# VectorE makes the inverse roots of the second layer's norms for the first four turns, in place of GpSimd

## The reference

```python
x = x + _L1_ffn_ref(_layernorm(x), ...)            # gates by attention over 524288 edges, 4 experts, 2 chosen
x = x + _L2_gnn_ref(_layernorm(x), adj, ...)       # inside: x + relu((adj @ h) @ W_rel + b + h @ W_root), h = layer_norm(x, gamma, beta)
x = x + _L2_ffn_ref(_layernorm(x), ...)            # a shared expert and 2 of 8 experts for each row
x = x + _L3_gnn_ref(_layernorm(x), mask, adj, W)
x = x + _L3_ffn_ref(_layernorm(x), ...)            # 2 of 8 experts for each row
def _layernorm(x): return (x - mean(x)) / sqrt(var(x) + 1e-5)
```

## Time and profile before

| | |
|---|---|
| time, median of 3 runs | 2797.84 us (2797.29 to 2801.29) |
| the profiled execution | 2798.21 us, span 2796.4 us |
| mean granted TensorE clock | 0.897 of full speed |
| busy in the span: PE, DVE, ACT, POOL | 2234.9, 1778.3, 1368.1, 1307.3 us |

### The profile page before, as it was taken

The page is one execution under the profiler, slowest core; times in us unless marked ns, Lnnn a source line. Parts: engine busy times, 40 slices in busy tenths (PEclk is TensorE's granted clock), DMA queues, the critical chain, the costliest instruction groups (busy, mean ns, idle before and its releaser), DMA issues. The chain is left out here.

```text
span 2796.4 us, 40730 instructions
## 1 busy us (share of the span) xinstructions
PE 2234.9 (80%) x12080; PEld 1656.4 (59%) x12080; DVE 1778.3 (64%) x4734; ACT 1368.1 (49%) x3026; POOL 1307.3 (47%) x1219
## 2 busy tenths in 40 slices
PE   4989898999999897888605156588999989999990
PEld 2544545464555554655405155588988979889880
DVE  5999989777788575333476852766465585744512
ACT  3554647474756553555404053465546545444440
POOL 1011100100010575567755777416737767667776
PEclk9999999998999998999857577799999999999995
DMA  4010104000010214222231212345536554566662
GB/s 154 1 40 1 32 12 96 16 17 20 13 32 1 54 29 124 79 76 77 60 122 50 76 39 72 84 124 146 136 92 161 157 153 129 145 146 168 168 160 74
DMA packets 235651, 233.09 MB, mean 83 GB/s; under 512 B 60877, under 2 KB 185535, under 8 KB 234514
## 3 DMA queue, kind: packets, MB, share of 16 engines
q1 hardware_dynamic: 200626, 184.23, 22.6%
q0 software_dynamic: 34784, 46.03, 8.7%
HBM read 168.22 MB, written 68.45 MB: 85 GB/s over the span
## 5 line engine op out<-in xcount | busy, mean ns | idle before, releaser
L998 POOL TENSOR_TENSOR a_rstd<-a_var,minus_half 128x4 f32<-128x4 f32 x64 | 99.0, 1547 | 828.7 <-DVE a_var L1552 821.6
L2184 POOL DMA_INDIRECT c_slots<-sent,c_tokens_of_slots x340 | 355.4, 1045 | 236.0 <-issue 97.2
L1657 DVE TENSOR_TENSOR room<-room 128x768 f32<-128x768 f32 (+2 forms) x312 | 369.6, 1208 | 31.1 <-ACT room L1394 23.3
L2449 ACT ACTIVATE weights_f<-bank,c_expert 128x256 f32<-128x256 f32 x680 | 277.2, 471 | 207.5 <-PE bank L2230 207.1
L2230 PE MATMUL bank<-c_experts_w,weights_f 128*128 x2720 | 342.7, 281 | 24.1 <-ACT weights_f L2449 22.3
L2230 PEld LDWEIGHTS bank<-c_experts_w,weights_f 128*128 128x128 f32 x2720 | 331.5, 197 | 36.8 <-issue 33.5
L2230 PE MATMUL bank<-c_slots_t,c_expert 128*128 128x256 f32 x1360 | 338.6, 394 | 12.0 <-ACT weights_f L2449 5.4
L2230 PEld LDWEIGHTS bank<-c_slots_t,c_expert 128*128 128x128 f32 x1360 | 254.2, 197 | 48.3 <-issue 15.9
L1028 PE MATMUL bank<-a_h1p,weights_a 128*128 128x512 f32 x544 | 247.2, 605 | 2.3 <-ACT a_dist_exp L1371 2.3
L2646 DVE TENSOR_TENSOR c_made<-bank,c_expert 128x256 f32<-128x256 f32 x170 | 72.1, 424 | 239.0 <-PE bank L2230 221.4
L82 POOL DMA_INDIRECT got_room<-table_dram,own_rows x184 | 192.8, 1048 | 67.0 <-issue 66.7
(11 more groups left out here) (532 smaller groups left out, 4542.0 us busy)
## 6 DMA issues: line engine op xcount, KB each, us to landing
c_expert<-packed_dram SPq DMA_DIRECT2D x170, 322.0 KB, 3.4
made<-c_made SPq DMA_DIRECT2D x170, 128.0 KB
results_dram<-a_results SPq DMA_DIRECT2D x64, 256.0 KB, 2.2
room<-results_dram SPq DMA_DIRECT2D x16, 1024.0 KB, 6.8
room<-in_adj SPq DMA_DIRECT2D x32, 256.0 KB, 5.5
sent<-c_rows_to_send SPq DMA_DIRECT2D x32, 256.0 KB, 3.1
c_slots<-sent,c_tokens_of_slots POOLq DMA_INDIRECT x340
a_adj<-in_adj SPq DMA_DIRECT2D x16, 256.0 KB, 3.1
```

Of the source, the lines that this page charges most:

```text
L998: rstd.did(g_.tensor_tensor(st.rstd[:, :], st.var[:, :], env.minus_half[:, 0:GT], ALU.pow), what, k)
L1657: v.tensor_tensor((dv[:, :, 0, :], other(dv))[j], sv[:, :, 0, :], other(sv), (ALU.min, ALU.max)[j]).then_inc(sort_step, 1)
L2184: pool.indirect_dma_start(out=XS[p.r % S_BUFS][:, j, :], out_offset=None, in_=env.sent_dram[p.q], in_offset=bass.IndirectOffsetOnAxis(ap=T ...
L2449: go(H[p.m % 2][:, c, :], U[c // 2][:, (c % 2) * SLOT:(c % 2 + 1) * SLOT], func, bias=bias).then_inc(hidden, 1)
```

## The change

For `lift` of turns 0 to 3 and `settle` of groups 0 to 7 VectorE makes the inverse roots itself, with the integer first guess and three Newton steps of `inverse_root`, which the kernel already uses in its gates. The other norms (turns 4 to 7, and the third layer's `ease` and `blend`) stay on GpSimd. The tasks of these twelve norms lose their GpSimd step, `PREFER_C`, `SHARED_AFTER` (after how many slots the shared expert of each turn comes) and three assumed durations of `route` are other numbers, and so the orders of all five queues are computed anew.

```diff
-        if part and task.follows is not None and (task.follows, part) not in passed:
+        if part and task.follows is not None and part < len(tasks[task.follows].long) and (task.follows, part) not in passed:
...
-    "settle": [(DVE, 2.2), (POOL, 1.3)], "settle_end": ...
-    "route": [(DVE, 4.5), (ACTE, 0.3), (PE, 0.5), (DVE, 6.0)], ...
+    "settle": [(DVE, 2.2), (POOL, 1.3)], "lift_alone": [(DVE, 4.9)], "settle_alone": [(DVE, 4.2)], "settle_end": ...
+    "route": [(DVE, 6.2), (ACTE, 0.3), (PE, 0.6), (DVE, 7.3)], ...
...
+def rooted_by_vector(n, k):
+    return n == "lift" and k < TURNS // 2 or n == "settle" and k < GROUPS // 2
...
 PREFER_C = {  # all 43 pairs of numbers are replaced
-SHARED_AFTER = (0, 3, 6, 17, 19, 31, 40, 88)
+SHARED_AFTER = (0, 4, 6, 15, 17, 31, 40, 88)
...
-    return {(n, k): Task(LONG[n], ...
+    return {(n, k): Task(LONG[n + "_alone"] if rooted_by_vector(n, k) else LONG[n], ...
...
-    measured_at = {... if p[0] in NORMS)}
+    measured_at = {... if p[0] in NORMS and not rooted_by_vector(*p))}
...
+        ROOT_HALF, ROOT_SQUARE = sb("root_half", [P, 2 * PAIR]), sb("root_square", [P, 2 * PAIR])
...
-                v.tensor_scalar(VAR[r][:, 0:tall[what]], MV[r][:, :, 1], LN_EPS, None, ALU.add).then_inc(var_ready, 1)
+                ins = v.tensor_scalar(VAR[r][:, 0:tall[what]], MV[r][:, :, 1], LN_EPS, None, ALU.add)
+                if rooted_by_vector(what, k):
+                    link(ins)
+                    link(inverse_root(nc, link, RSTD[r][:, :], VAR[r][:, :], ROOT_HALF[:, 0:roots[what]], ROOT_SQUARE[:, 0:roots[what]]))
+                else:
+                    ins.then_inc(var_ready, 1)
...
-                dve.wait_ge(rstd_ready, inverted_at[what, k])
+                if not rooted_by_vector(what, k):
+                    dve.wait_ge(rstd_ready, inverted_at[what, k])
```

More of the change, by code:

```diff
@@ L1880 @@
     "adj": [(PE, 0.6), (ACTE, 0.75)], "xt": [(PE, 0.6), (ACTE, 0.75)], "agg": [(PE, 1.35), (ACTE, 0.7)], "conv": [(PE, 2.2)],
-    "settle": [(DVE, 2.2), (POOL, 1.3)], "settle_end": [(DVE, 0.2), (ACTE, 1.95)], "f2_xt": [(PE, 0.6), (ACTE, 0.75)], "f2_score": [(PE, 0.9), (DVE, 0.3)],
-    "route": [(DVE, 4.5), (ACTE, 0.3), (PE, 0.5), (DVE, 6.0)], "mark": [(DVE, 3.0), (PE, 0.9)], "list": [(DVE, 0.3)], "save": [(SP, 0.5)], "pull": [(POOL, 2.6)], "gather": [(POOL, 5.2)], "gather_last": [(POOL, 5.2)],
+    "settle": [(DVE, 2.2), (POOL, 1.3)], "lift_alone": [(DVE, 4.9)], "settle_alone": [(DVE, 4.2)], "settle_end": [(DVE, 0.2), (ACTE, 1.95)], "f2_xt": [(PE, 0.6), (ACTE, 0.75)], "f2_score": [(PE, 0.9), (DVE, 0.3)],
+    "route": [(DVE, 6.2), (ACTE, 0.3), (PE, 0.6), (DVE, 7.3)], "mark": [(DVE, 3.0), (PE, 0.9)], "list": [(DVE, 0.3)], "save": [(SP, 0.5)], "pull": [(POOL, 2.6)], "gather": [(POOL, 5.2)], "gather_last": [(POOL, 5.2)],
     "load3": [(SP, 2.0)], "back": [(DVE, 4.5)], "ease": [(DVE, 2.6), (POOL, 1.9)], "ease_end": [(DVE, 2.2)],
@@ L1891 @@
 NORMS = ("lift", "settle", "ease", "blend")
+def rooted_by_vector(n, k):
+    return n == "lift" and k < TURNS // 2 or n == "settle" and k < GROUPS // 2
 WHOLE_C = ("edge", "late", "route")
 PREFER_C = {
-    "adj": (-29.0, 1806.0), "agg": (603.0, 292.0), "back": (2080.0, -19.0), "blend": (3135.0, 364.0), "blend_end": (1193.0, 105.0),
-    "climb": (-1245.0, 825.0), "compare": (3094.0, 286.0), "conv": (-659.0, -1286.0), "ease": (-198.0, -554.0), "ease_end": (-2050.0, 2075.0),
-    "edge": (2854.0, 1748.0), "enter_end": (-133.0, 29.0), "experts": (1239.0, -3046.0), "f2_score": (-355.0, 1770.0), "f2_xt": (-135.0, 421.0),
@@ L1897 @@
[L1897 to L1900, removed]
@@ L1901 @@
-    "pull": (-110.0, -1483.0), "raise": (3303.0, 1605.0), "route": (43.0, 1909.0), "rows": (-1056.0, 1024.0), "save": (-857.0, 2844.0),
-    "settle": (409.0, -825.0), "settle_end": (899.0, 868.0), "soften": (2618.0, 1044.0), "store": (-1967.0, 56.0), "sum": (-4725.0, -651.0),
-    "take": (1010.0, 2409.0), "xt": (-4171.0, 2182.0)}
-SHARED_AFTER = (0, 3, 6, 17, 19, 31, 40, 88)
+    "adj": (2678.0, 1757.0), "agg": (245.0, -281.0), "back": (209.0, 1695.0), "blend": (6614.0, 2584.0), "blend_end": (3809.0, -667.0),
@@ new lines @@
+    "climb": (-2301.0, -351.0), "compare": (8690.0, 1389.0), "conv": (-993.0, -1266.0), "ease": (-249.0, -785.0), "ease_end": (-2478.0, 188.0),
+    "edge": (6737.0, 1108.0), "enter_end": (-2571.0, 455.0), "experts": (3490.0, -3063.0), "f2_score": (-85.0, 1811.0), "f2_xt": (1266.0, 2121.0),
+    "f3_score": (879.0, 1916.0), "f3_xt": (-282.0, 725.0), "fetch": (9325.0, 1593.0), "flip": (1061.0, 613.0), "g3_xt": (800.0, 3086.0),
+    "gather": (-3141.0, -3187.0), "gather_last": (-6639.0, -2102.0), "late": (-3173.0, 5092.0), "leave": (1348.0, 721.0), "lift": (195.0, 166.0),
@@ new lines @@
+    "lift_end": (2119.0, -4496.0), "list": (4672.0, -2013.0), "load2": (6460.0, -2093.0), "load3": (-1563.0, -663.0), "lower": (-182.0, -218.0),
+    "mark": (1528.0, 1502.0), "mask": (-398.0, 4046.0), "mix": (2448.0, -2538.0), "project": (-263.0, -76.0), "pt": (4960.0, 1358.0),
+    "pull": (955.0, -186.0), "raise": (1298.0, -47.0), "route": (-612.0, 2528.0), "rows": (-1958.0, -1290.0), "save": (2922.0, 1214.0),
+    "settle": (-1629.0, 1013.0), "settle_end": (1245.0, -1994.0), "soften": (2292.0, 3535.0), "store": (-1377.0, 1473.0), "sum": (-2463.0, 3314.0),
@@ L1907, in mark_list @@
+    "take": (3415.0, 1623.0), "xt": (-2945.0, 4425.0)}
+SHARED_AFTER = (0, 4, 6, 15, 17, 31, 40, 88)
 def mark_list():
@@ L1994, in work_c @@
     totals.update({n: len(passes) for n in ("raise", "lower", "take")})
-    return {(n, k): Task(LONG[n], needs[n](k), LANDS.get(n, 0.0), (n, k - 1) if k else None) for n in needs for k in range(totals[n])}
+    return {(n, k): Task(LONG[n + "_alone"] if rooted_by_vector(n, k) else LONG[n], needs[n](k), LANDS.get(n, 0.0), (n, k - 1) if k else None) for n in needs for k in range(totals[n])}
 def phase_c(nc, env):
@@ L2010, in phase_c @@
     at_c = offsets(W_C)[0]
-    measured_at = {piece: n + 1 for n, piece in enumerate(p for p in orders[DVE] if p[0] in NORMS)}
+    measured_at = {piece: n + 1 for n, piece in enumerate(p for p in orders[DVE] if p[0] in NORMS and not rooted_by_vector(*p))}
     factors_at = {piece: n + 1 for n, piece in enumerate(p for p in orders[DVE] if p[0] in ("lift_end", "settle_end"))}
```

## The result

The changed kernel took 2809.29 us (median of 11 runs, 2803.28 to 2813.92), the kernel before 2798.44 us (11 runs): ratio 1.0037, 95% interval 1.0026 to 1.0047, so 10.4 us slower. I had forecast 2790 us, 8.2 us faster. The time lies inside the range, on the other side of "before", near the third rival's 2812 us. The profiled execution of the changed kernel took 2809.29 us, its span is 2807.5 us.

What follows compares the result with a forecast made beforehand. VectorE was taken to bound 1440 to 1586 us, GpSimd's gathers 1586 to 1751, TensorE mostly after 1825. Old order +0.8 and new order -9 gave -8.2 us against 2798.2: 2790 us, range 2770 to 2812.

Steps and rivals of the forecast that it cites:

- third rival: VectorE's added first-stage instructions cost their full time, no waits shortened: +13.8 us, 2812 us; chance 0.24.
- first stage: 1440 to 1586 us, VectorE fullest: 18.0 us added, 12 won back, so 6.0 us longer.
- On the path, with the order as it is: Sum over the stages before the gates with queue orders kept: gates start 1.8 us later.
- 12 of the 16.8 us: VectorE's first-stage waits for TensorE, claimed to shrink by 12 us as factors follow roots sooner; bounds 0 and 16.8.
- my sum: Old-order terms +0.8 us (gates +1.8, stall -1.0) and new order -9 us: -8.2 us.
- the new order: Replanned queues use a third of GpSimd's 26.9 us of waits for variances: -9 us, bounds 0 and -26.9.
- second stage: 1586 to 1751 us, GpSimd fullest: losing its roots saves 4.8 us; group 7's root before the gates adds 0.6.
- The stall: VectorE's 21.55 us wait until 1751.03 for a settle's root: becomes another wait, worth only 1.0 us.
- The warning at the end of the prediction: If gates and end move opposite ways, the order after 1825 or GpSimd's tail, left at zero, decided it.
- Slower: VectorE's added instructions in the first stage stand in full: Rival: the 16.8 us of VectorE waits are not shortened; +13.8 us, 2812 us; chance 0.24.
- Gathers held: Rival: each of 144 new VectorE instructions holds GpSimd's gathers 0.17 us, 24.5 us in all; 2814 us; chance 0.03.

Runs made afterwards that it cites:

- e2: Against the kernel before: all twelve roots on VectorE, every queue's order kept; ratio 1.0071, +19.9 us.
- e5: Against the kernel before: twelve roots on VectorE, old order, but each norm's factors moved right behind its roots; ratio 1.0055, +15.4 us.
- e6: Against the kernel before: only the seven early roots (lifts 0 to 2, settles 0 to 3) on VectorE, old order; ratio 1.0091, +25.5 us.
- e4: Against the kernel before: only the five late roots (lift 3, settles 4 to 7) on VectorE, old order; ratio 0.9982, -5.0 us.
- e9: Against the kernel before: five late roots on VectorE, old order, with these norms' factors moved right behind their roots; ratio 0.9980, -5.6 us.
- e14: Against the kernel before: all roots on GpSimd, queues in the new order up to about 1790 us, then the old order; ratio 1.0023, +6.4 us.
- e11: Against the kernel before: all roots on GpSimd, old queues up to about 1825 us, new preferences from there on; ratio 1.0047, +13.2 us.
- e13: Changed kernel's roots and queues up to about 1790 us, then the order of the kernel before; ratio to before 1.0019, +5.3 us.
- e7: Changed kernel with one Newton step in place of three in each of the twelve roots; ratio to the kernel before 1.0034, +9.5 us.

## Why the prediction was wrong

**The failed step is the first stage of "On the path, with the order as it is".** "I take 12 of the 16.8 us as won back ... The stage is 18.0 - 12 = 6.0 us longer." With the order kept nothing was won back (16.8 us of waits in e2), and even with the factors moved it was 4.5 us (e5). The reason that I gave for the 12 was that the factors would follow the roots at once, and I put it into the part in which the order is as it is, where they can't: their place in VectorE's queue is behind the pair's edges. In the changed kernel, whose order is new, the first lift's factors are also 13 us behind. So a gain of order was counted in a sum that keeps the order. The cost itself was right within 1.3 us: 18.0 us counted, 19.3 measured.

Without the 12 us my sum puts the gates at 1.8 + 12 = 13.8 us later (this was the third rival), and e2 has them 13.0 us later in the phase. That the two agree to a microsecond is partly luck: the first stage is 19.5 us longer and not 18.0, and between it and the gates 6.5 us come back and not 4.2. The end, however, is 19.9 us later. And the 12 us are not the whole miss: without them the sum is +12.8 - 9 = +3.8 us, 6.6 us short of the measured 10.4.

**A second fault made this worse: I priced the end by the gates alone.** I had written that what counts is "when half 1's edges end and how much of TensorE's work is done by then", and then worked out only the first. The first list decides when TensorE gets its first slots, and it is 19.5 us later in e2 and 24.2 us later in the changed kernel. There the gates come 21 us earlier and TensorE still has 6.2 us less done by 1825. In the five kernels that keep the old order the end lies near 0.6 of the sum of both shifts: 19.5, 25.7, 13.9, -4.9 and -4.3 us for e2, e6, e5, e4 and e9, measured 19.9, 25.5, 15.4, -5.0 and -5.6 us. The factor is an estimate of mine, fitted to these five afterwards. In the new order it fails: it gives +1.9 us for the changed kernel and -2.9 us for e14, measured 10.4 and 6.4 us. So in the old order the two milestones give the price of a change of placement, and the new order has a cost of its own that neither shows.

**Right at the end: the second stage.** -4.8 + 0.6 - 1.0 = -5.2 us; e4 measured -5.0 (interval -8.7 to -1.7). The stall turned into other waits of the same length, as the paragraph on it said. On the way the sum is less good: its gates are 4.2 us earlier, measured 8.0. One microsecond of that is a misread row: 1751.98 in the earlier trace rows is not when pair 15's data came, since what released it is VectorE's own L140, which stood behind the stall.

**Right in size, for the pair: the new order.** I gave it -9 us; from e2 to the changed kernel it is 19.9 - 10.4 = 9.5 us. It is luck and not a confirmation of how I came to it, a third of GpSimd's 26.9 us: those waits turned into waits for rooms (65.8 us against 33.8), and the same order costs 15.4 us when GpSimd makes the roots, and behind 1825, where I had left it at zero, it costs e11 13.2 us. The warning at the end of the prediction, that gates and end may move apart, is what happened. That the order after 1825 or the tail then decided it holds only in part: 5.3 of the 10.4 us are there without the new order behind 1790 (e13).

**The rivals.** "Slower: VectorE's added instructions in the first stage stand in full" is the one that the runs bear out for the roots (e2, e6), with 6.9 us more on the way from the gates to the end in e2. "Gathers held" is not: the gathers' line in the changed kernel has the median of the earlier trace rows or less, with VectorE busier beside them, and its 184 gathers are busy 190.0 us in all, against 192.8 us before.

```profile
L82 POOL DMA_INDIRECT got_room<-table_dram,own_rows x184: 992/997/1877, 1427.7 to 1738.7; - x184
```

The Trainium skill, page "SBUF — State Buffer" (section "SBUF: two separate sides"), speaks of VectorE keeping GpSimd off a shared port in its two-port modes; these instructions, on 4 and 16 numbers, show nothing of it here. No trace shows whether they ran in such a mode.

**A kernel that beats both.** e4_roots_late and e9_late_behind, with the roots of lift 3 and settles 4 to 7 on VectorE and all queues as before, take 0.18% and 0.20% less than before and some 0.55% less than the changed kernel (0.9982 and 0.9980 against 1.0037). This is the change made only where GpSimd is the fuller engine.

**Open.** Why shorter roots (e7) brought no measurable time in the changed kernel, though its list and gates came earlier; how the new order's loss behind 1825 divides over its waits; and where e14 loses its 6.4 us, with list, gates and TensorE's work by 1825 about as before or better. No run shortened the roots in the old order, where list and gates do tell the end.

## What to carry to other kernels

Moving work from one engine to another helped here in the stage in which the first is the fuller and cost where the other is: the same move of 2.6 us instructions was worth -5 us behind 1586 and +25 us ahead of it, so do it by stage. A wait shrinks only if what it waits for really starts earlier: before it is counted as won back, look at what stands between producer and consumer in the same queue. And with a planned order, judge a change of placement and a change of order apart: the same new order costs 15.4 us with the old placement and gives 9.5 us back with the new one. An early milestone (the gates, 21 us early in the phase) may be bought with one that matters as much (the first list, 24 us late).

## What the hardware showed that I had not expected

The part ahead of `phase_c`, which none of these runs is meant to change, is not equally long in every profiled execution: the first pair of half 1 began at 1442.45 us in the changed kernel and at 1435.04 in e13, whose queues are the same up to there, and the runs of the kernel before spread from 2786.73 to 2802.05 us on one chip. Milestones of two traces may be compared to a few microseconds only when their common start is taken off.
